# A 64-expert layer on one core: shared experts as split one-pass products in two halves, four memory rows per token

## The chip, the cores and the metric

The kernel runs on one core of a Trainium2 chip. The metric is the device time of one execution in microseconds (us). Its engines work side by side, each through its own list of instructions: PE (TensorE, matrix products), ACT (ScalarE), DVE (VectorE), POOL (GpSimd) and SP (SyncE, which only issues transfers). They wait for each other through semaphores. SBUF is the on-chip memory of 128 partitions, PSUM the banks that PE writes, DRAM the memory of the chip.

## The reference

A decoder of two layers on x of 4 x 512 tokens of width 512. The part that is changed is the feed-forward of the first layer:

```python
b, t, d = x.shape                      # B, T, D = 1, 512 x 4 tokens here, 512
E, K, F, S, SF, CAP = 64, 4, 128, 2, 512, 64
logits = flat @ router_w.T
scores = jax.nn.softmax(logits, axis=-1)
_, topk_idx = jax.lax.top_k(logits + router_bias, K)
topk_w = jnp.take_along_axis(scores, topk_idx, axis=-1)
topk_w = topk_w / topk_w.sum(axis=-1, keepdims=True)
# each expert takes its first CAP tokens: tok_table (E, CAP), w_table (E, CAP)
xg = flat[tok_table]
y = jnp.einsum('ecf,edf->ecd', silu(xg @ gate_w) * (xg @ up_w), down_w)
out = zeros.at[tok_table].add(y * w_table[..., None])
# two shared experts of width 512, for every token
sg = jnp.einsum('nd,sfd->nsf', flat, sh_gate_w)
su = jnp.einsum('nd,sfd->nsf', flat, sh_up_w)
out = out + jnp.einsum('nsf,sdf->nd', silu(sg) * su, sh_down_w)
x = layernorm(x + out)
```

Before it stand a gated linear recurrence and a layer of token-id experts, after it window attention, a product in an 8-bit format and a latent attention with eight experts.

## The kernel before

The program runs its stages one after the other; `moe_layer` is the third. Names in it: `B` = 4 groups of 512 tokens, 16 `TILES` of 128 tokens, `KD` = 4 slices of the width 512, `KF` = 4 slices of the shared width, `PAIRS` = 32 pairs of experts (two experts of 64 slots fill the 128 rows of one product), `K_C` = 4 experts per token.

*The shared experts.* Their work is cut into 64 steps, 8 for each of 8 units; a unit is one group of 512 tokens with one shared expert (`unit // SHARED` is the group). The first 4 steps of a unit are gate/up steps: 4 products of 128x512 for gate and 4 for up, in f32; ACT takes tanh of the gate (`shared_gate`), DVE makes the hidden product of it in two operations, `gu_s` and `hs`. The other 4 are down steps: 4 products each for one tile of 128 tokens, and one DVE operation that adds the result to that tile's rows (`row`). Steps 0 to 19 (`EARLY_STEPS`) come before the expert pairs, while the tokens are being routed; steps 20 to 47 are dealt out among the pairs (`middle`); steps 48 to 63 (`LATE`) come after the last pair.

*Routing.* For each group PE turns x (`turn_batch`, copied from PSUM by ACT into `xT`), computes the router's `logits`, and counts with `places` how many earlier tokens chose an expert. DVE does the rest in three parts: `pick` (four largest), `choose` (masks) and `share_out` (softmax weights, slots and addresses). POOL then writes 16 times 128 entries of (token, row of the sums, weight) into the table `slots` in DRAM by indirect transfers (L1210), four in flight at a time. The order on DVE is written out by hand: `share_out(2)` follows step 5, `share_out(3)` step 9, so that of the early steps 10 remain after it.

*The pairs.* When all 64 scatters have landed, SP reads the table back (`of_slot`, L1180), and POOL gathers for each pair its 128 rows of x (`gather`, L1222), two pairs ahead. On PE the loop is software-pipelined, with `middle` steps of the shared experts between:

```python
for q in range(-2, PAIRS + 1):
    if q + 2 < PAIRS: turn(q + 2)
    for n in middle.get(q, []): shared_step(n)
    if 0 <= q + 1 < PAIRS: gates(q + 1)
    if 0 <= q < PAIRS: turn_hidden(q)
    if 0 <= q - 1: down(q - 1)
```

The experts' weights come through a ring of four buffers of 1.5 MB; SP asks for pair q's when `down(q - 4)` is done. ACT scales a pair's result y by the slots' weights (`result`, L1297) and POOL scatters it with adding into `expert_sums` in DRAM (`add_rows`, L1230), two rows per token (a token's row is 2 * token + half, where half tells experts of one parity from the other's); each scatter waits for the one before. `expert_sums` is zeroed in the first stage by one transfer (L263).

*The end.* After the last scatter SP loads the sums in 6 transfers of up to three tiles (L1193), DVE adds the two rows of a token to its own (`sum_rows`, L1589 and L1590), takes mean and variance (`spread`), POOL the power -0.5, and ACT normalises. The tiles are taken between the late steps (`tiles_at`).

What sets the order is the text alone: each engine does its list as written, and there is no planner.

## Time and profile before

| | |
|---|---|
| time, median of 3 runs | 2373.93 us (2370.86 to 2379.55) |
| the profiled execution: its time | 2381.64 us |
| the profiled execution: its span | 2379.9 us |
| mean granted clock of PE | 0.951 |
| busy: PE, DVE, ACT, POOL | 90%, 57%, 34%, 28% of the span |
| the 64-expert stage | about 481 to 982 us of the span |
| its rows of the page: f32 products gate, up, down | 256 each, 115.4, 115.1 and 114.0 us busy |
| scatters with adding (L1230) | 32, of 1570 ns each on POOL |
| ring loads of 1536 KB | 32, 7.0 us from issue to landing |
| loads of the sums of 1536 KB | 5 (and a smaller one), 9.9 us |
| zeroing of the sums, 8192 KB | 1, 27.5 us |

Times inside the trace count from the start of the span. A window's row gives the busy time of each engine in a stretch and the number of its instructions; where PE's busy time equals the stretch, PE sets its length. The page counts a PE instruction as busy from its own start to a modelled end, and instructions overlap, so the step from one start to the next is read from the timeline instead. The granted clock is a share of full speed.

### The profile page before, as it was taken

The numbers are of one execution on the slowest core, as the hardware profiler recorded it, in microseconds if no ns is written. First come the engines' busy times: TensorE is split into PE (matmuls) and PEld (weight loads), VectorE is DVE, ScalarE is ACT, GpSimd is POOL, SyncE is SP. The second block draws the span as 40 slices with busy tenths as digits, with TensorE's granted clock in tenths as the row PEclk, the third lists the DMA queues.
The fourth block names the chain that finished last, engine by engine and source line by source line (L and its number), as shares of the span: only waits on it lengthen the run. The fifth ranks groups of instructions, "written<-read, shape, count | busy, mean of one in ns | idle before, by whom it ended". The sixth has DMA issues, their size and how long they took to land. (4 is left out here: it accounts for less than half of the span.)

```text
span 2379.9 us, 31463 instructions
## 1 busy us (share of the span) xinstructions
PE 2139.5 (90%) x10918; PEld 1180.7 (50%) x10919; DVE 1362.7 (57%) x3185; ACT 806.4 (34%) x1333; POOL 674.3 (28%) x945
## 2 busy tenths in 40 slices
PE   9999979979999999879999988578888888889994
PEld 5777748755444443445555543233333333336763
DVE  5866768846121226566777774845656565445443
ACT  5554624420112211333444433533322232123333
POOL 1200015516433321223343433011113131214553
PEclk9999989979999999998999997789999999999997
DMA  7211232270177764363333330200000000065555
GB/s 268 75 36 54 89 121 82 94 290 1 28 240 248 244 210 152 100 134 81 81 88 82 88 68 1 97 3 1 2 19 2 19 28 19 19 177 159 100 99 171
DMA packets 101178, 230.31 MB, mean 97 GB/s; under 512 B 18886, under 2 KB 42626, under 8 KB 93870
## 3 DMA queue, kind: packets, MB, share of 16 engines
q1 hardware_dynamic: 78478, 186.61, 25.3%
q0 software_dynamic: 22560, 41.87, 7.9%
q8 instruction: 83, 1.36, 0.2%
q14 instruction: 57, 0.47, 0.1%
HBM read 169.45 MB, written 63.53 MB: 98 GB/s over the span
## 5 line engine op out<-in xcount | busy, mean ns | idle before, releaser
L2137 DVE CUSTOM_DVE_ANT_0 D_ps<-D_ps,D_mask 128x256 f32<-128x256 f32 (+1 forms) x512 | 186.6, 419 | 61.9 <-PE D_ps L2033 60.6
L1859 POOL TENSOR_SCALAR_AFFINE_SELECT D_probs<-D_probs 128x256 f32<-128x256 f32 x256 | 106.4, 422 | 288.2 <-ACT D_probs L1917 288.1
L1917 ACT ACTIVATE D_probs<-D_ps 128x512 f32<-128x512 f32 (+1 forms) x256 | 125.4, 543 | 184.4 <-PE D_ps L2055 184.3
L3170 DVE TENSOR_REDUCE F_neg_max<-F_ps 128x4 f32<-128x2048 f32 (+1 forms) x64 | 93.9, 1488 | 107.3 <-PE F_ps L3068 101.2
L2920 ACT ACTIVATE F_probs<-F_ps 128x1536 f32<-128x1536 f32 (+1 forms) x48 | 76.4, 1591 | 186.9 <-PE F_ps L3084 186.9
L1393 PE MATMUL C_ps<-C_down_shared,C_hs 128*128 128x512 f32 x256 | 114.0, 594 | 2.5 <-DVE C_hs L1560 1.5
L1381 PE MATMUL C_ps<-C_xT,C_gate_shared 128*128 128x512 f32 x256 | 115.4, 593 | 0.5 <-ACT C_xT L1256 0.5
L1381 PE MATMUL C_ps<-C_xT,C_up_shared 128*128 128x512 f32 x256 | 115.1, 592 | 0.0
L2033 PE MATMUL D_ps<-D_k_stack,D_q_stack 96*128 96x256 bf16 (+1 forms) x512 | 94.2, 270 | 15.2 <-DVE D_maxima L2137 11.8
L1230 POOL DMA_INDIRECT expert_sums<-C_y,C_of_slot x32 | 50.2, 1570 | 173.0 <-ACT C_y L1297 107.9
L2801 POOL TENSOR_SCALAR_AFFINE_SELECT F_probs<-F_probs 128x512 f32<-128x512 f32 x64 | 41.1, 654 | 180.5 <-ACT F_probs L2920 180.5
L3486 POOL DMA_INDIRECT choice_sums<-G_y,G_sum_at x38 | 65.9, 1734 | 88.7 <-DMA choice_sums<-G_y,G_sum_at 76.2
L2055 PE MATMUL D_ps<-D_q_stack,D_k_stack 99*128 99x256 bf16 (+1 forms) x512 | 76.8, 276 | 14.8 <-DMA D_q_stack<-D_m_lo 14.8
L1210 POOL DMA_INDIRECT slots<-C_entry,C_address x64 | 66.0, 1031 | 76.4 <-DVE C_address L1545 40.1
L2072 PE MATMUL D_ps<-D_probs,D_v 128*32 128x256 f32 (+1 forms) x1024 | 78.6, 380 | 6.0 <-POOL D_probs L1861 3.3
L1381 PEld LDWEIGHTS C_ps<-C_xT,C_up_shared 128*128 128x128 f32 x256 | 48.6, 190 | 61.2 <-issue 61.0
L1861 POOL TENSOR_SCALAR_AFFINE_SELECT D_probs<-D_probs 128x256 f32<-128x256 f32 x192 | 78.8, 410 | 0.0
L1393 PEld LDWEIGHTS C_ps<-C_down_shared,C_hs 128*128 128x128 f32 x256 | 47.1, 190 | 57.2 <-issue 52.6
L2033 PEld LDWEIGHTS D_ps<-D_k_stack,D_q_stack 96*128 96x128 bf16 x512 | 39.4, 101 | 72.7 <-DVE D_maxima L2137 34.7
L1274 ACT ACTIVATE C_th_s<-C_ps 128x512 f32<-128x512 f32 x32 | 19.1, 597 | 165.0 <-PE C_ps L1381 165.0
L1381 PEld LDWEIGHTS C_ps<-C_xT,C_gate_shared 128*128 128x128 f32 x256 | 47.2, 190 | 54.2 <-issue 54.2
L1553 DVE SCALAR_TENSOR_TENSOR C_gu_s<-C_th_s,C_ps 128x512 f32<-128x512 f32 x32 | 22.0, 686 | 90.3 <-ACT C_th_s L1274 90.2
(574 smaller groups left out, 4947.7 us busy)
## 6 DMA issues: line engine op xcount, KB each, us to landing
C_ring<-moe_experts_dram SPq DMA_DIRECT2D x32, 1536.0 KB, 7.0
qk_parts<-D_parts SPq DMA_DIRECT2D x32, 384.0 KB, 2.6
expert_sums<-A_zeros SPq DMA_DIRECT2D x1, 8192.0 KB, 27.5
C_ring<-expert_sums SPq DMA_DIRECT2D x5, 1536.0 KB, 9.9
D_q_stack<-qk_parts SPq DMA_DIRECT2D x16, 384.0 KB, 4.7
D_k_stack<-qk_parts SPq DMA_DIRECT2D x16, 384.0 KB, 7.7
B_w<-ctxT_dram SPq DMA_DIRECT2D x1, 4096.0 KB, 16.8
B_c<-ctx_dram SPq DMA_DIRECT2D x4, 1024.0 KB, 8.2
```

What stands on the lines that cost most here:

```text
L1210: pool.indirect_dma_start(slots, bass.IndirectOffsetOnAxis(ap=address[:, b, k, t:t + 1], axis=0), entry[:, b * GROUP + t, k, :], None, bou ...
L1381: last = nc.tensor.matmul(ps[:, bank + part, :], w_shared[part][:, k, f:f + P], xT[:, k, g * S:(g + 1) * S], start=(k == 0), stop=(k == KD ...
L1393: last = nc.tensor.matmul(ps[:, 2 + c % 2, :], hs[:, m, i * P:(i + 1) * P], down_shared[:, s * KF + m, :], start=(m == 0), stop=(m == KF - 1))
L1859: last = nc.gpsimd.affine_select(now[:, :, 0:P], now[:, :, 0:P], [[0, 2], [1, P]], ALU.is_ge, 0.0, base=0, channel_multiplier=-1)
L1861: last = nc.gpsimd.affine_select(now[:, :, P:2 * P], now[:, :, P:2 * P], [[0, 2], [-1, P]], ALU.is_ge, 0.0, base=0, channel_multiplier=1)
L1917: nc.scalar.activation(probs[at % 2][:, 2 * pair:2 * pair + 2, 0:w], ps[:, 4 + unit % 3, :].rearrange("p (h q) -> p h q", h=2)[:, :, 0:w], ...
L2033: last = nc.tensor.matmul(ps[:, 2 + u % 2, h * 256 + first:(h + 1) * 256], q_stack[0:STACK, head, t * P:(t + 1) * P], k_stack[0:STACK, hea ...
L2055: last = nc.tensor.matmul(bank[:, h * 256:h * 256 + w], k_stack[:, head, kb * P:(kb + 1) * P], q_stack[:, head, kb * P:kb * P + w], start= ...
L2072: last = nc.tensor.matmul(ps[h * (P // 4):(h + 1) * (P // 4), 7, kb * P:kb * P + w], v[b % 2][:, kb, first:first + 2 * DK], probs[at % 2][ ...
L2137: last = nc.vector.tensor_tensor_reduce(now, now, mask[:, first:256], 1.0, -3e38, ALU.add, ALU.max, maxima[n % 2][:, head, t:t + 1])
L2920: nc.scalar.activation(probs[u][:], ps[:, 0:GROUP, 0:WIDTH[u]], ACT.Exp, scale=1.0 / np.sqrt(HD)).then_inc(exp_ready, 1)
L3170: last = nc.vector.tensor_reduce(neg_max[n % 2][:, :, t], ps[:, 0:GROUP, at:at + w], AX_X, ALU.max, negate=True)
```

## The change

The two shared experts are treated as one of width 1024, in two halves of 512: units 0 to 3 are the first half with groups 0 to 3, units 4 to 7 the second half (`half, g = divmod(unit, B)`).
SBUF holds the weights of one half at a time and x for two groups at a time. The second halves are loaded over the first between the ring's loads (q == 6 and 11), rounded at q == 6 and 10. x is written out to DRAM (`spill_x`, 2 MB for each of 4 groups) and brought back for the second half (`bring_x`).

The transposes of groups 2 and 3 move in between the early steps, and with them their logits, `pick`, `choose` and `share_out` move back. There are 24 early steps; the others are dealt out anew over the pairs.

`expert_sums` has four rows per token (4 * token + k), each written once, so the scatter neither adds nor waits for the one before; the zeroing is twice as large. At the end 16 loads of 1 MB replace 6 of up to 1.5 MB; POOL adds rows 2 and 3 to rows 0 and 1 (`halve`), then DVE adds both to the token's row as before.

The core of the diff:

```diff
@@ rglru_layer, SP
-                         zeros[:].unsqueeze(1).to_broadcast([P, 2 * TILES, D])).then_inc(zeroed, 16)
+                         zeros[:].unsqueeze(1).to_broadcast([P, K_C * TILES, D])).then_inc(zeroed, 16)
@@ moe_layer
-EARLY_STEPS = 20
+EARLY_STEPS = 24
...
-    for n in range(EARLY_STEPS, LATE):
-        middle.setdefault((n - EARLY_STEPS) * PAIRS // (LATE - EARLY_STEPS), []).append(n)
+    HALF = STEPS // 2
+    for n in range(EARLY_STEPS, HALF):
+        middle.setdefault(n - EARLY_STEPS + (-1 if n < HALF - KF else 0), []).append(n)
+    for n in range(HALF, LATE):
+        middle.setdefault(8 + (n - HALF) * (PAIRS - 8) // (LATE - HALF), []).append(n)
+    SECOND_GATES, SECOND_DOWN = 6, 10
...
@@ SP
+            def load_weights(half, *parts):
+                for part in parts:
+                    if half:
+                        sp.wait_ge((gate_s, up_s, down_s)[part], B * KF)
+                        sp.wait_ge(w_lo_ready[part], 1)
...
+                    sp.dma_start(w_raw[part][:], source).then_inc(w_in[part], 16)
+            def spill_x(b):
+                sp.wait_ge(x_hi_ready, KD * (b + 1))
+                sp.dma_start(x_spill[b, 0], x_hi[b % 2][:].bitcast(F32).rearrange("p k n -> p (k n)")).then_inc(spilled[b % 2], 16)
+                sp.wait_ge(x_lo_ready, b + 1)
...
+            def bring_x(g):
+                sp.wait_ge(up_s, (B + g - 1) * KF)
+                sp.wait_ge(spilled[g % 2], 2 * 32)
...
+            load_weights(0, 0, 1, 2)
             for q in range(RING):
...
+            for b in range(B):
+                spill_x(b)
             sp.wait_ge(scattered, 16 * K_C * TILES)
             sp.dma_start(of_slot[:].rearrange("p n o -> p (n o)"), slots.rearrange("(p n) o -> p (n o)", p=P)).then_inc(slots_in, 16)
+            bring_x(0)
             for q in range(RING, PAIRS):
+                if q == 6:
+                    load_weights(1, 0, 1)
+                    bring_x(1)
+                if q == 11:
+                    load_weights(1, 2)
+                if q == 16:
+                    bring_x(2)
+                if q == 28:
+                    bring_x(3)
...
+            for t in range(TILES):
+                if t >= HOMES:
+                    sp.wait_ge(summed, t - HOMES + 1)
+                sp.dma_start(homes[:, t % HOMES].rearrange("p c n -> p (c n)"),
+                             sums.rearrange("(t p c) d -> p t (c d)", p=P, c=K_C)[:, t, :]).then_inc(sums_in[t % HOMES], 16)
@@ POOL
             def add_rows(q):
                 pool.wait_ge(y_ready, q + 1)
-                if q >= 1:
-                    pool.wait_ge(stored[(q - 1) % 2], 16 * ((q - 1) // 2 + 1))
...
-                                        bounds_check=last_sum, oob_is_err=False, compute_op=ALU.add).then_inc(stored[q % 2], 16)
+                                        bounds_check=last_sum, oob_is_err=False).then_inc(stored[q % 2], 16)
+            def halve(t):
+                pool.wait_ge(sums_in[t % HOMES], 16 * (t // HOMES + 1))
+                nc.gpsimd.tensor_tensor(homes[:, t % HOMES, 0:2, :], homes[:, t % HOMES, 0:2, :], homes[:, t % HOMES, 2:4, :], ALU.add
+                                        ).then_inc(halved, 1)
@@ ACT
                 for k in range(KD):
                     act.wait_ge(x_turned, b * KD + k + 1)
-                    nc.scalar.copy(xT[:, k, b * S:(b + 1) * S], ps[:, 4 + k % 2, :]).then_inc(xT_ready, 1)
+                    nc.scalar.copy(x_raw[b % 2][:, k, :], ps[:, 4 + k % 2, :]).then_inc(x_raw_ready, 1)
+                    nc.scalar.copy(x_hi[b % 2][:, k, :], ps[:, 4 + k % 2, :]).then_inc(x_hi_ready, 1)
+            def high_of_hidden(m):
+                act.wait_ge(hs_raw_ready, m + 1)
+                nc.scalar.copy(hs_hi[:, m % KF, :], hs_raw[:, m % KF, :]).then_inc(hs_hi_ready, 1)
...
@@ PE
+                        pe.wait_ge(w_hi_ready[part], half + 1)
                         for k in range(KD):
-                            last = nc.tensor.matmul(ps[:, bank + part, :], w_shared[part][:, k, f:f + P],
-                                                    xT[:, k, g * S:(g + 1) * S], start=(k == 0), stop=(k == KD - 1))
+                            nc.tensor.matmul(ps[:, bank + part, :], w_hi[part][:, k, now], x_hi[j][:, k, :], start=(k == 0), stop=False)
...
+                            nc.tensor.matmul(ps[:, bank + part, :], w_hi[part][:, k, now], x_lo[j][:, k, :], start=False, stop=False)
...
+                            last = nc.tensor.matmul(ps[:, bank + part, :], w_lo[part][:, k, now], x_hi[j][:, k, :], start=False,
+                                                    stop=(k == KD - 1))
...
-            turn_batch(2)
-            turn_batch(3)
             pe.wait_ge(converted, 1)
             places(0)
             for n in range(EARLY_STEPS):
                 shared_step(n)
                 if n == 1:
                     places(1)
-                if n == 2:
+                if n == 4:
+                    turn_batch(2)
+                if n == 6:
                     logits(2)
-                if n == 5:
+                if n == 10:
                     places(2)
-                if n == 7:
+                if n == 12:
+                    turn_batch(3)
+                if n == 14:
                     logits(3)
-                if n == 9:
+                if n == 18:
                     places(3)
@@ DVE
+            def low_of_hidden(m):
+                dve.wait_ge(hs_hi_ready, m + 1)
+                nc.vector.tensor_tensor(hs_lo[:, m % KF, :], hs_raw[:, m % KF, :], hs_hi[:, m % KF, :].bitcast(F32), ALU.subtract
+                                        ).then_inc(hs_lo_ready, 1)
             def shared_step(n):
                 unit, down, i = step_of(n)
+                if i or down:
+                    if not down or i == 0:
+                        low_of_hidden(unit * KF + (KF if down else i) - 1)
...
             choose(0)
+            low_x(0)
             pick(1)
+            low_of_weights(0, 0, 1)
             share_out(0)
             shared_step(0)
             choose(1)
             shared_step(1)
             share_out(1)
+            low_of_weights(0, 2)
             shared_step(2)
...
+            low_x(1)
+            for n in range(3, EARLY_STEPS):
                 shared_step(n)
+                if n == 8:
+                    pick(2)
+                    low_x(2)
+                if n == 9:
+                    choose(2)
+                if n == 11:
+                    share_out(2)
+                if n == 16:
+                    pick(3)
+                    low_x(3)
+                if n == 17:
+                    choose(3)
+                if n == 19:
+                    share_out(3)
...
@@ program
-    expert_sums = nc.dram_tensor("expert_sums", (2 * TOKENS, D), F32).ap()
+    expert_sums = nc.dram_tensor("expert_sums", (K_C * TOKENS, D), F32).ap()
```

## Rows read from the trace of the kernel before

**Rows 1.** Windows: us, busy PE PEld DVE ACT POOL, clock, DMA share, GB/s

```profile
480.80:517.00 36.20, 27.55 (x131) 24.61 (x131) 12.25 (x51) 10.74 (x24) 0.34 (x3) 0.55 0.99 368
517.00:635.90 118.90, 117.96 (x327) 56.10 (x328) 63.89 (x171) 9.02 (x20) 67.93 (x66) 1.00 0.11 38
635.90:896.00 260.10, 257.15 (x1121) 115.85 (x1121) 52.55 (x136) 53.03 (x107) 76.54 (x60) 1.00 0.69 220
896.00:981.70 85.70, 83.15 (x194) 36.20 (x192) 52.74 (x104) 15.57 (x23) 6.84 (x6) 1.00 0.30 105
```

**Rows 2.** Timeline of PE, gate products of two steps: start, us, engine, line, operation

```profile
607.27 3.60 PE L1381 MATMUL C_ps<-C_xT,C_gate_shared 128*128 128x512 f32 x8
...
614.14 3.60 PE L1381 MATMUL C_ps<-C_xT,C_gate_shared 128*128 128x512 f32 x8
```

**Rows 3.** Timeline of PE, one-pass products in the first stage

```profile
213.63 1.33 PE L435 MATMUL A_ps<-A_u_lo,A_wa_hi 128*128 128x512 f32 x5
214.79 1.32 PE L429 MATMUL A_ps<-A_u_hi,A_wa_hi 128*128 128x512 f32 x5
```

**Rows 4.** Groups by line, later stages: busy us, mean ns, idle before

```profile
L2195 DVE TENSOR_TENSOR D_wv_lo<-D_wv,D_wv_hi 128x2048 fp32r<-128x2048 f32 x1 | 2.3, 2293 | 1.1 <-ACT D_wv_hi L1934 1.1
...
L3528 ACT CAST G_x_hi<-G_xgT 128x512 fp32r<-128x512 f32 x38 | 23.6, 620 | 7.1 <-DVE G_xgT L3753 6.5
...
L3759 DVE TENSOR_TENSOR G_x_lo<-G_xgT,G_x_hi 128x512 fp32r<-128x512 f32 x38 | 26.3, 693 | 24.8 <-ACT G_x_hi L3528 24.7
```

**Rows 5.** Timeline of PE, the second group's logits

```profile
502.50 7.09 PE L1353 MATMUL C_ps<-C_router,C_xT 128*128 128x64 f32 x32 [0.68 <-ACT C_xT L1256]
```

**Rows 6.** Timeline of DVE: first operations of share_out(0), choose, step 1, share_out(1), step 2

```profile
512.05 1.23 DVE L1517 TENSOR_TENSOR C_picked<-C_chosen,C_expd 128x1024 f32<-128x1024 f32 x1
...
524.93 0.17 DVE L1497 CAST C_at<-C_best_at 128x16 f32<-128x16 uint32 x1
...
529.22 0.69 DVE L1553 SCALAR_TENSOR_TENSOR C_gu_s<-C_th_s,C_ps 128x512 f32<-128x512 f32 x1
...
531.79 1.22 DVE L1517 TENSOR_TENSOR C_picked<-C_chosen,C_expd 128x1024 f32<-128x1024 f32 x1
...
539.51 0.68 DVE L1553 SCALAR_TENSOR_TENSOR C_gu_s<-C_th_s,C_ps 128x512 f32<-128x512 f32 x1
```

**Rows 7.** Timeline from the last group's first scatter to the first gather

```profile
600.23 0.97 POOL L1210 DMA_INDIRECT slots<-C_entry,C_address  x1 [1.39 <-DMA slots<-C_entry,C_address]
...
624.76 0.33 SPq L1180 DMA_DIRECT2D C_of_slot<-slots  x1
...
627.25 0.98 POOL L1222 DMA_INDIRECT C_xg<-x,C_of_slot  x1 [3.64 <-DMA C_of_slot<-slots]
```

**Rows 8.** DMA issues, the gathers: median us from issue to landing

```profile
C_xg<-x,C_of_slot POOLq DMA_INDIRECT x32, 5.1
```

**Rows 9.** Windows with full queues and in the middle of the pairs

```profile
910.00:925.00 15.00, 15.00 (x36) 6.63 (x35) 10.17 (x20) 1.19 (x2) 0.00 (x0) 1.00 0.99 397
...
700.00:750.00 50.00, 50.00 (x218) 22.60 (x216) 9.46 (x25) 10.90 (x22) 17.87 (x14) 1.00 0.88 282
```

**Rows 10.** Windows in the second stage, PE idle and the 4 us after

```profile
334.00:346.00 12.00, 0.34 (x2) 0.34 (x3) 1.91 (x5) 0.00 (x0) 4.85 (x6) 0.57 0.59 219
346.00:350.00 4.00, 4.00 (x15) 3.25 (x14) 1.38 (x2) 1.17 (x2) 0.68 (x2) 0.58 0.82 191
```

**Rows 11.** Timeline of SP, the issue of the loads of the sums

```profile
908.44 23.52 SPq L1193 DMA_DIRECT2D C_ring<-expert_sums  x6
```

**Rows 12.** Timeline of POOL and DVE, two additions that overlap

```profile
1660.96 1.27 POOL L2795 TENSOR_TENSOR F_plain<-F_raw,F_rope 128x512 f32<-128x512 f32 x1 [5.46 <-ACT F_raw L2860]
1661.59 1.18 DVE L3153 TENSOR_TENSOR F_full<-F_full,F_plain 128x512 f32<-128x512 f32 x1
```

**Rows 13.** Group of DVE's first additions of the sums in the last stretch

```profile
L1589 DVE TENSOR_TENSOR rows<-rows,C_ring 128x512 f32<-128x512 f32 x16 | 11.0, 689 | 4.6 <-DMA C_ring<-expert_sums 4.2
```

**Rows 14.** Waits of SP's queue after the zeroing: us in all, count, longest

```profile
SPq L252 <- PE A_ps L435: 114.1, 2, 61.6
```

More of the change, by code:

```diff
@@ L1085, in moe_layer @@
     LATE = STEPS - LATE_UNITS * 2 * KF
-    LOADS = [range(i, min(i + 3, TILES)) for i in range(0, TILES, 3)]
+    HOMES = 6
     def step_of(n):
@@ L1132, in moe_layer @@
         share, place, kept, slotf, drop = (sb(n, [P, K_C, GROUP]) for n in ("share", "place", "kept", "slotf", "drop"))
-        sloti, pairi, half = (sb(n, [P, K_C, GROUP], I32) for n in ("sloti", "pairi", "half"))
-        twice = sb("twice", [P, TILES], I32)
+        sloti, pairi = (sb(n, [P, K_C, GROUP], I32) for n in ("sloti", "pairi"))
         address = sb("address", [P, B, K_C, GROUP], I32)
@@ L1266, in shared_gate @@
                 unit, down, i = step_of(n)
+                if i or down:
+                    if not down or i == 0:
+                        high_of_hidden(unit * KF + (KF if down else i) - 1)
                 if not down:
@@ L1366, in shared_step @@
                 unit, down, i = step_of(n)
-                g, s = divmod(unit, SHARED)
+                half, g = divmod(unit, B)
+                j = g % 2
                 if not down:
@@ L1385, in shared_step @@
                     c = unit * KF + i
-                    if n == KF:
-                        pe.wait_ge(down_in, 16)
+                    now = slice(i * P, (i + 1) * P)
                     if c >= 2:
                         pe.wait_ge(added, c - 1)
+                    pe.wait_ge(w_hi_ready[2], half + 1)
                     for m in range(KF):
-                        pe.wait_ge(hs_ready, unit * KF + (m + 1 if i == 0 else KF))
-                        last = nc.tensor.matmul(ps[:, 2 + c % 2, :], hs[:, m, i * P:(i + 1) * P],
-                                                down_shared[:, s * KF + m, :], start=(m == 0), stop=(m == KF - 1))
+                        pe.wait_ge(hs_hi_ready, unit * KF + (m + 1 if i == 0 else KF))
+                        nc.tensor.matmul(ps[:, 2 + c % 2, :], hs_hi[:, m, now], w_hi[2][:, m, :], start=(m == 0), stop=False)
+                    pe.wait_ge(w_lo_ready[2], half + 1)
+                    for m in range(KF):
+                        nc.tensor.matmul(ps[:, 2 + c % 2, :], hs_hi[:, m, now], w_lo[2][:, m, :], start=False, stop=False)
+                    for m in range(KF):
+                        pe.wait_ge(hs_lo_ready, unit * KF + (m + 1 if i == 0 else KF))
+                        last = nc.tensor.matmul(ps[:, 2 + c % 2, :], hs_lo[:, m, now], w_hi[2][:, m, :], start=False, stop=(m == KF - 1))
                     last.then_inc(down_s, 1)
@@ L1604, in _ @@
             nc.vector.memset(so_far[:], 0.0)
-            nc.vector.tensor_scalar(twice[:], myself[:], 2, None, ALU.mult)
+            for k in range(K_C):
+                nc.vector.tensor_scalar(entry[:, :, k, 1], myself[:], K_C, k, ALU.mult, ALU.add)
             nc.vector.tensor_copy(entry[:, :, :, 0], myself[:].unsqueeze(2).to_broadcast([P, TILES, K_C]))
```

180 lines of the change are left out of this document (108 added, 72 removed).

## The prediction

> **What bounds the kernel now.** I read the page's shares first (PE 90% busy), then the windows of the 64-expert stage, since an average over stages says nothing of one. The reader is to see that PE is the limit in three of its four stretches [rows 1]: 117.96 of 118.90 us busy in the early one, 257.15 of 260.10 in the one with the expert pairs, 83.15 of 85.70 in the last. Only the front, 36.20 us with DMA at a share of 0.99, waits for data. So a cheaper product shortens a stretch only as far as nothing else becomes late in it. The chain of waits ends in the latent stage and does not reach this one; I therefore took the order of the work on each engine from the code and the durations from the timeline and the groups by line, and last looked for what the trace shows of a DMA at its limit and of POOL beside DVE.
>
> **The change part by part.** *The products.* A gate/up step of 16 f32 products takes 614.14 - 607.27 = 6.87 us [rows 2], a down step of 8 half of it, 3.43. Five f32r products of the same shape take 214.79 - 213.63 = 1.16, or 0.233 each [rows 3]. So 24 of them are 5.59, 12 are 2.80: 1.28 and 0.63 less. With 32 steps of each kind PE has 61 us less to do. Where that is worth something is the question in each stretch.
>
> *Front and early steps: +45.* Each group's logits need both copies of x (0.62 each on ACT [rows 4]); I put the end of logits(1), 502.50 + 7.09 = 509.59 before [rows 5], at 512.5, two pairs of copies of 1.46 later. From there DVE's list is serial: pick 2.3 (2.46 from 509.59 to 512.05, less the signal [rows 5, 6]), two lows of weights 4.6 (2.29 each [rows 4]), share_out 7.7 (531.79 to 539.51 [rows 6]), step 0 1.4, choose 4.3 (524.93 to 529.22 [rows 6]), step 1 2.1, share_out 7.7, low of down 2.3, step 2 2.1, low of x 2.3, step 3 2.1; a step is two operations, from step 1 on three, of 0.69 [rows 4]. That is 38.9: DVE is through step 3 at 551.4, and with the rounding on ACT and the wait signals PE begins step 4 at 552.3. PE's own steps 0 to 3 are 22.4, so it waits some 13 us there, before the first down step.
> Steps 4 to 19 are 8 x 5.59 + 8 x 2.80 = 67.1, the logits of groups 2 and 3 7.4 (7.09 at a clock near half, about 3.6 at full, an estimate [rows 5]), their transposes, moved in from the front, 7.0 (per group four of the eight copies of 0.62 before PE may fill the banks again, and its own 1.0), places 0.6. Step 12 needs the low of step 11's result, which stands on DVE behind share_out(2): 6.5 of its 7.7 show. Less 0.7 hidden under the copies: 87.9, step 19 ends at 640.2. Now comes what I hold to be the main loss: share_out(3) stands behind step 19 (before: step 9). Its addresses are there at 640.2 + 0.9 + 7.7 = 648.8. The 16 scatters of a group took 624.76 - 600.23 = 24.5 [rows 7]; SP's load of the slots follows at once, the gather 2.5 later (627.25), and a gather lands 5.1 after its issue [rows 8]. Turn(0) comes at 648.8 + 24.5 + 2.5 + 5.1 = 680.9 instead of 635.9. PE has only steps 20 to 23 (11.2) to cover it, is done at about 658 and idles 23. Bounds: without any of the waits on DVE the early steps end 15 us earlier (+30); with the clock falling in each wait, as below, +54.
>
> *Pairs: -23.7.* 12 gate steps x 1.28 and 12 down steps x 0.63 save 15.4 and 7.6, and the early part has taken over four down steps: 13.7. Sum 36.7. The turns, gates and downs of the pairs themselves stay as they are. Against the gain: between gates(5) and gates(6) SP must now also bring the second gate and up halves and a group of x, 2 x 1.05 and 2 x 1.05 MB beside ring loads of 1.57 MB each: 7.3 MB at the 397 GB/s seen with the queues full [rows 9] is 18.5 us and about 2 of latency, against some 14 us of PE's work that covers it (three pairs' own 3.7, that is 257.15 less 12 x 6.87 and 16 x 3.43 over 32, and a down step): 7 us. The x of groups 2 and 3 costs about 1.5 each, for the ring is four deep and refills behind it. And PE comes out of its 23 us of idling at a low clock: after 12 us with hardly any PE work the granted clock was 0.57, near the lower of its two levels (1.2 of 2.4 GHz), and the next 4 us ran at 0.58 although PE was busy throughout [rows 10]; that is about 2 us lost after each long wait, 3 in all. -36.7 + 10 + 3 = -23.7. In total the stretch must carry 44.0 (ring) + 3.1 + 8.4 (x) + 8.4 (gathers) + 8.4 (scatters) = 72.3 MB: 182 us at 397 GB/s, but 226 at 320 GB/s, the rate that a full share would have given in the middle of the pairs (282 at 0.88 [rows 9]). So ends: -36.7 (nothing waits) to 0 (no more than the 282 itself: 256 us, and the clock's 3). I take -23.7, near the end that the chain of PE's own work gives, since at the share of 0.88 PE was busy for all 50.00 of 50.00 us; the scatters without adding need no wait for the one before and cost nothing here, since y's release is hidden behind PE.
> The Trainium skill ("SBUF — State Buffer", "Summary: rules for kernel authors") reckons 358 GB/s between HBM and SBUF; the row of 397 differs and decides. By the page's figure the 7.3 MB would take 20.4 us, an estimate, and the sum would be 2 us higher.
>
> *Late steps: +20.3.* The scatters end sooner: no chain of waits, so the first sums can be asked for some 8 us after the last pair instead of 12.4 (908.44 - 896.0 [rows 1, 11]). A tile is 1 MB now, POOL halves it: twice the elements of its 128x512 addition of 1.27 [rows 12], 2.5 us; the first tile is ready at about +13. Then there are 16 halvings = 40.5 and 32 additions on DVE of 0.69 = 22 [rows 13], the lows of hidden 3.4. When POOL and a DVE operation with two SBUF inputs run at once they do not share: the DVE addition that began 0.63 us into POOL's 1.27 took 1.18 instead of 0.69, that is, it ended 0.54 after POOL had [rows 12, 13]. Taken as exclusion the three add up to 66, with DVE's remaining work between to 75; from the last tile's sum to the end of the stage are 18 for the last down steps, spreads and normalising. 13 + 75 + 18 = 106 against 85.7. Bounds: if POOL and DVE share, PE alone is left, with 8 x 1.28 + 8 x 0.63 = 15.3 less to do (-15); if every halving also delays the gate steps' operations that PE waits for, 16 x 1.0 more, +36. The 16 MB of sums need 42 us at 397 GB/s and stay under POOL's pace.
> The Trainium skill ("SBUF — State Buffer", "Who interferes with whom") says that a DVE operation with two SBUF inputs and a GpSimd one that reads SBUF hold the shared read for the whole instruction, whoever begins first. The row of 1.18 agrees; were the price always that row's 0.49, 40 such operations would cost 20 us, and late would come to +11.
>
> *The rest.* Zeroing doubles to 16 MB: by the page 8 MB landed in 27.5 us; SP's next step after it has a wait of 61.6 us [rows 14], which hides 27.5 more. Weights' first halves are 3 MB less ahead of the ring in the front; it stays with the transposes and ACT.
>
> Sum: +45 - 23.7 + 20.3 = +41.6, to the profiled execution's 2381.64: 2423.2. The median of the runs shown, 2373.93, lies 7.7 below that execution, so I predict 2416.
>
> **The rivals.** *POOL and DVE share after all.* For it: 1.18 is one row, and tiles may queue so that the two alternate. Against it: all 16 halvings fall into the stretch with 32 additions. Then a quarter of PE's 15.3 shows in the late steps, no more, for DVE's 52.74 [rows 1] grow by 5.5 of lows and stand right behind PE: -4, sum +17.3: 2391. *DMA binds the pairs.* For: share 0.88 in the middle already [rows 9] and now 72.3 MB in 236.4 us, 306 GB/s where 220 were asked for [rows 1]. Against: the 397 with big transfers. At 282 the stretch goes to about 260 instead of 236.4: 2440. *Gains and waits cancel.* DVE's early list is half as costly as I make it and the pairs keep 33 of their 36.7: +25 - 33 + 8: 2374. *Faster.* One mechanism: PE alone decides. Its place is turn(0); it decides as soon as steps 4, 12 and 20 find their operands ready. Then only the distance of share_out(3) from turn(0) is left (32 us of scatters, load and gather against 11.2 of PE's work, +22), the pairs give all 36.7 and the late steps 10 of their 15.3: -25, about 2349. For it: PE is the limit in three stretches now. Against it: DVE's list of 38.9 us beside 22.4 of PE's work.
>
> **How the numbers follow.** Forecast 0.40 (2416, alone 2400 to 2432); POOL and DVE share 0.22 (2391); DMA binds 0.12 (2440); cancel 0.13 (2374); faster 0.13 (2349). The range is 2352 to 2445: it leaves out about half of the faster case and half of the DMA case. Within 0.5%, some 12 us, a measurement can't tell from no change. The cancelling case is the one that lies there; so faster 0.13, same 0.13, slower 0.74.
>
> **What would show it.** The products: step time 5.6 on PE with f32r. Early: PE idle before the first down step released by DVE's lows or ACT's hs, share_out(3) ending near 649, and PE idle before turn(0) released by the gather, some 23 us. Pairs: idle before gates(6) released by the ring's DMA, none elsewhere over 3 us. Late: halvings of 2.5 us or more, DVE additions of up to 3 us that end just after a halving, the last tile's sum about 88 us after the last pair. I am wrong if turn(0) comes before 660, if additions stay at 0.69 beside POOL, or if the pairs' stretch keeps its 260.

## The result, and the profile after

The changed kernel takes 2433.92 us (median of 4 runs, 2424.17 to 2443.09), the kernel before beside it 2375.30: 1.0246 times as long, with an interval of 1.0201 to 1.0292. That is 18 us more than the 2416 forecast and inside the range. The profiled execution took 2443.09 us, the longest of the four.

I cut the stage at four starts on PE: its first transposes, turn(0), the down products of the last pair, and the next stage's first product. The lengths between them, in us, for every kernel of this study; each ratio is to runs of the kernel before that were timed beside that kernel, whose median moves by a few us (2372.78 beside e10, 2377.56 beside e9):

| kernel | front and early, to turn(0) | pairs | last stretch | time, median | ratio to before |
|---|---|---|---|---|---|
| before | 149.1 | 259.1 | 92.1 | 2375.30 | |
| changed | 196.2 | 252.2 | 107.6 | 2433.92 | 1.0246 |
| e1 routing earlier | 172.1 | 251.4 | 107.9 | 2412.67 | 1.0162 |
| e2 DVE halves | 196.5 | 250.9 | 105.1 | 2429.36 | 1.0213 |
| e3 loads spread | 193.5 | 238.7 | 105.9 | 2419.06 | 1.0177 |
| e4 two rows again | 195.9 | 267.9 | 92.2 | 2429.51 | 1.0232 |
| e5 four rows alone, on before | 139.9 | 259.1 | 102.8 | 2386.30 | 1.0045 |
| e6 = e2, order of sums | 195.0 | 255.6 | 96.6 | 2420.85 | 1.0190 |
| e7 = e1 + e3 | 171.9 | 240.1 | 106.7 | 2396.51 | 1.0092 |
| e8 all, and two more edits | 166.7 | 230.3 | 97.4 | 2373.80 | 0.9992 |
| e9 = e8, four tiles on PE | 166.7 | 228.3 | 99.0 | 2372.54 | 0.9982 |
| e10 = e9, last sums earlier | 167.3 | 227.0 | 94.9 | 2370.11 | 0.9982 |

So the changed kernel loses 47.1 us before turn(0), gains 6.9 in the pairs and loses 15.5 in the last stretch: +55.7; 1.9 more come ahead of the stage and 3.6 after it, which makes the 61.1 between the two spans (2441.0 and 2379.9). Each length is of one execution. Where kernels of the table share a stretch's instructions, it differs by up to 3.0 us in the first column (changed, e2, e3, e6), 4.7 in the second (changed, e1, e2, e6) and 2.0 in the third (changed, e1, e3, e7), so a smaller difference shows nothing. What follows the stage takes 1383.8 to 1396.4 us in them, though nothing was changed in it.

The windows of the three stretches of the changed kernel, columns as in [rows 1], which they answer:

```profile
488.60:684.80 196.20, 143.60 (x633) 117.36 (x633) 101.15 (x239) 39.54 (x75) 66.65 (x66) 0.82 0.32 122
684.80:936.95 252.15, 226.18 (x1229) 141.21 (x1229) 64.46 (x147) 64.64 (x122) 59.84 (x60) 0.95 0.72 264
936.95:1044.57 107.62, 75.74 (x293) 58.80 (x293) 82.16 (x117) 21.40 (x33) 48.25 (x24) 0.83 0.41 161
```

PE fills none of the three any more: it idles 52.6, 26.0 and 31.9 us. Its products did get cheaper. Two gate steps that follow each other on its timeline (start, duration) are 5.44 us apart, where [rows 2] have 6.87:

```profile
943.53 1.07 PE L1471 MATMUL C_ps<-C_x_hi,C_gate_hi 128*128 128x512 f32 x4
...
948.97 1.07 PE L1471 MATMUL C_ps<-C_x_hi,C_gate_hi 128*128 128x512 f32 x4
```

PE's waits in the early part, in order: for choose(1), for the last hidden product before the first down step, for the lows behind share_out(2) and share_out(3), and for the first gather:

```profile
532.59 0.40 PE L1448 MATMUL C_ps<-C_mask,C_before 128*128 128x256 bf16 x1 [5.71 <-DVE C_so_far L1612]
...
551.16 0.80 PE L1490 MATMUL C_ps<-C_down_hi,C_hs_hi 128*128 128x512 f32 x1 [3.74 <-ACT C_hs_hi L1327]
...
602.76 0.80 PE L1496 MATMUL C_ps<-C_down_hi,C_hs_lo 128*128 128x512 f32 x1 [5.21 <-DVE C_hs_lo L1660]
...
651.56 0.80 PE L1496 MATMUL C_ps<-C_down_hi,C_hs_lo 128*128 128x512 f32 x1 [5.21 <-DVE C_hs_lo L1660]
...
684.78 1.11 PE L1506 MATMUL C_ps<-ident,C_xg 128*128 128x128 f32 x4 [22.60 <-DMA C_xg<-x,C_of_slot]
```

The chain to that gather, from the timelines of DVE, POOL and SP, answers to [rows 7]: last address at 650.72, first scatter, table, first gather 28 us after the address.

```profile
650.72 0.17 DVE L1646 TENSOR_TENSOR C_address<-C_sloti,C_drop 128x16 int32<-128x16 int32 x1
```

```profile
651.66 0.97 POOL L1256 DMA_INDIRECT slots<-C_entry,C_address  x1 [24.38 <-DVE C_address L1646]
...
678.64 0.98 POOL L1268 DMA_INDIRECT C_xg<-x,C_of_slot  x1 [3.70 <-DMA C_of_slot<-slots]
```

In the pairs PE has three long waits for the ring. Its timeline, with one product that did not wait (755.66) between; the trace names no releaser ("issue"), but SP's timeline, below it, shows what stood ahead of the ring's load:

```profile
747.28 3.68 PE L1517 MATMUL C_ps<-C_ring,C_xgT 128*64 128x256 f32 x16 [10.29 <-issue]
...
755.66 1.95 PE L1517 MATMUL C_ps<-C_ring,C_xgT 128*64 128x256 f32 x16
...
825.82 3.68 PE L1517 MATMUL C_ps<-C_ring,C_xgT 128*64 128x256 f32 x16 [5.38 <-issue]
...
912.13 3.21 PE L1517 MATMUL C_ps<-C_ring,C_xgT 128*64 128x256 f32 x14 [4.58 <-issue]
```

```profile
723.13 0.38 SPq L1198 DMA_DIRECT2D C_gate_raw<-moe_sh_gate_dram  x1
723.61 0.45 SPq L1198 DMA_DIRECT2D C_up_raw<-moe_sh_up_dram  x1
724.15 2.56 SPq L1209 DMA_DIRECT2D C_x_hi<-x_spill  x1
726.76 1.69 SPq L1210 DMA_DIRECT2D C_x_lo<-x_spill  x1
...
806.46 0.38 SPq L1209 DMA_DIRECT2D C_x_hi<-x_spill  x1
...
893.69 0.38 SPq L1209 DMA_DIRECT2D C_x_hi<-x_spill  x1
```

After such a wait the same 16 products take 3.68 us instead of 1.95, as in [rows 10]: the granted clock was 0.50 in the 4 us from 747.28, after 10.29 us of idling, and 1.00 from 751.30 on. In the last stretch DVE's additions of the sums take up to 2.77 us while POOL halves, and 0.68 when it does not (POOL's list pauses from 968.4 to 972.6); these rows, from the timelines of POOL and DVE, answer to [rows 12, 13]:

```profile
946.69 7.67 POOL L1291 TENSOR_TENSOR C_homes<-C_homes 128x1024 f32<-128x1024 f32 x3 [6.70 <-DMA C_homes<-expert_sums]
954.92 13.45 POOL L1291 TENSOR_TENSOR C_homes<-C_homes 128x1024 f32<-128x1024 f32 x5 [0.56 <-DMA C_homes<-expert_sums]
```

```profile
949.96 2.15 DVE L1707 TENSOR_TENSOR rows<-rows,C_homes 128x512 f32<-128x512 f32 x1
952.15 2.77 DVE L1708 TENSOR_TENSOR rows<-rows,C_homes 128x512 f32<-128x512 f32 x1
...
969.97 0.68 DVE L1707 TENSOR_TENSOR rows<-rows,C_homes 128x512 f32<-128x512 f32 x1
```

### The profile page after: what moved, and what is told of

Same layout as the page of the kernel before. It is cut to its first block and busy times, and to the rows that moved or that the text cites. A ratio compares the mean times of both kernels' runs of the same rounds, so it can differ in the third digit from the quotient of the medians.

```text
span 2441.0 us, 32391 instructions
## 1 busy us (share of the span) xinstructions
PE 2098.7 (86%) x11299; PEld 1266.2 (52%) x11303; DVE 1427.1 (58%) x3222; ACT 841.3 (34%) x1387; POOL 695.4 (28%) x961
## 5 line engine op out<-in xcount | busy, mean ns | idle before, releaser
L1517 PE MATMUL C_ps<-C_ring,C_xgT 128*64 128x256 f32 x512 | 67.3, 408 | 22.2 <-issue 20.5
L1273 POOL DMA_INDIRECT expert_sums<-C_y,C_of_slot x32 | 32.6, 1019 | 167.4 <-ACT C_y L1371 167.4
L2265 DVE DVE_READ_ACCUMULATOR2_ANT D_maxima<- 128x1 f32 x512 | 72.6, 142 | 0.0
L3781 PE MATMUL G_ps<-G_w_down,G_hidT 128*128 x152 | 71.5, 593 | 0.9 <-ACT G_hidT L3663 0.9
L2183 PEld LDWEIGHTS D_ps<-D_q_stack,D_k_stack 99*128 99x128 bf16 x512 | 42.7, 101 | 52.5 <-issue 23.0
L3127 PE MATMUL F_ps<-F_wo,F_oT 128*128 128x512 f32 x128 | 63.3, 622 | 6.0 <-DVE F_raw L3344 3.0
L1685 DVE SCALAR_TENSOR_TENSOR rows<-C_ps,rows 128x512 f32<-128x512 f32 x32 | 22.1, 691 | 78.4 <-PE C_ps L1496 76.4
L2145 PE MATMUL D_ps<-D_wo,D_oT 128*128 128x512 f32 x128 | 66.5, 621 | 0.2 <-ACT D_oT L2034 0.2
L1490 PE MATMUL C_ps<-C_down_hi,C_hs_hi 128*128 128x512 f32 x128 | 42.5, 442 | 27.3 <-ACT C_hs_hi L1327 26.3
```

What stands on the lines that cost most here:

```text
L1517: last = nc.tensor.matmul(ps[e * CAP:(e + 1) * CAP, 5, 0:2 * F_C], xgT[q % 2][:, k, e * CAP:(e + 1) * CAP], ring[q % RING][:, e, k * 2 * F ...
L2145: last = nc.tensor.matmul(ps[:, bank, :], oT[t][:, k, :], wo[:, k, :], start=(k == 0), stop=(k == KD - 1))
L2183: last = nc.tensor.matmul(bank[:, h * 256:h * 256 + w], k_stack[:, head, kb * P:(kb + 1) * P], q_stack[:, head, kb * P:kb * P + w], start= ...
L2265: last = nc.vector.tensor_tensor_reduce(now, now, mask[:, first:256], 1.0, -3e38, ALU.add, ALU.max, maxima[n % 2][:, head, t:t + 1])
L3781: last = nc.tensor.matmul(ps[:, 6 + a, :], hidT[a][:, m, :], w_down[:, bass.ds(e, 1), m, :], start=(m == 0), stop=(m == MF - 1))
```

## The experiments

**e1: the routing of groups 2 and 3 earlier.** Shown for group 3; group 2 and `exponentials` on ACT move likewise.

```diff
@@ PE
-                if n == 14:
+                if n == 13:
                     logits(3)
-                if n == 18:
+                if n == 15:
                     places(3)
...
@@ DVE
-                if n == 16:
+                if n == 13:
                     pick(3)
...
-                if n == 17:
+                if n == 14:
                     choose(3)
-                if n == 19:
+                if n == 15:
                     share_out(3)
...
```

> Only the order of the routing of groups 2 and 3 changes: logits, pick, choose and share_out of group 2 after steps 5, 5, 6 and 7, of group 3 after steps 13, 13, 14 and 15 (in the changed kernel after 6, 8, 9, 11 and 14, 16, 17, 19). Theory: turn(0) waits for the last group's addresses, which stood behind step 19. Then the addresses are there some 30 us earlier (about 620), the waits for lows at steps 12 and 20 (6.5 each) go, PE's idle time before turn(0) falls from 22.6 to under 10 us, turn(0) comes near 654 instead of 684.8, and the kernel is about 30 us faster than the changed one (2404). Rival: the gain is given back in the pairs' loads, since the ring's transfers bind there: then the pairs' stretch grows from 253 by what turn(0) gains, and the kernel stays within 8 us of 2434.

Turn(0) came 24.1 us nearer to the stage's start (196.2 to 172.1), not 30, and PE still waits 11.4 there, more than the 10 I allowed: the steps before it became shorter by the same edit, so there was less to cover the scatters. The pairs kept their length (251.4), with the first wait for the ring as long as ever. The theory holds in its cause and overstated the size: the median is 21.3 us below the changed kernel's, where 30 were expected. The rival falls. The rows, PE's timeline of e1:

```profile
660.15 1.11 PE L1506 MATMUL C_ps<-ident,C_xg 128*128 128x128 f32 x4 [11.39 <-DMA C_xg<-x,C_of_slot]
...
722.53 3.68 PE L1517 MATMUL C_ps<-C_ring,C_xgT 128*64 128x256 f32 x16 [10.24 <-issue]
```

**e2: DVE halves.**

```diff
@@ DVE, sum_rows; POOL's halve goes
-dve.wait_ge(halved, t + 1)
+dve.wait_ge(sums_in[t % HOMES], 16 * (t // HOMES + 1))
+steps.after(nc.vector.tensor_tensor(homes[:, t % HOMES, 0:2, :], homes[:, t % HOMES, 0:2, :], homes[:, t % HOMES, 2:4, :], ALU.add))
```

> Only who halves the four rows changes: DVE adds rows 2 and 3 to rows 0 and 1 itself (one 128x1024 operation of about 1.25 us a tile) and POOL does nothing but the powers. Theory: POOL's halving and DVE's additions exclude each other, so moving the work to the engine that waits costs less than it frees: the additions fall from up to 2.77 us to 0.69, the last stretch from 102 to 85 to 95 us, the kernel is 8 to 17 us faster than the changed one. Rival: POOL's help is real and DVE becomes the bound: 16 x 1.25 = 20 us more on DVE, the last stretch grows by 5 to 15.

Neither came: the last stretch went from 107.6 to 105.1. The groups of DVE by line, of the changed kernel and then of e2 (busy us, mean ns), say why:

```profile
L1708 DVE TENSOR_TENSOR rows<-rows,C_homes 128x512 f32<-128x512 f32 x16 | 23.4, 1466 | 0.5
L1707 DVE TENSOR_TENSOR rows<-rows,C_homes 128x512 f32<-128x512 f32 x16 | 20.1, 1254 | 0.4
```

```profile
L1696 DVE TENSOR_TENSOR C_homes<-C_homes 128x1024 f32<-128x1024 f32 x16 | 19.6, 1223 | 0.4
L1697 DVE TENSOR_TENSOR rows<-rows,C_homes 128x512 f32<-128x512 f32 x16 | 11.1, 692 | 0.6
L1698 DVE TENSOR_TENSOR rows<-rows,C_homes 128x512 f32<-128x512 f32 x16 | 11.1, 692 | 0.5
```

Beside POOL the additions are busy 43.5 us, alone 22.2: POOL's 41 us of halving cost DVE 21.3, and doing it itself costs DVE 19.6. POOL's help is worth next to nothing: the 2.5 us are little more than the 2.0 by which equal stretches differ. What both kernels share is DVE's one list, which in e2 runs for 70.8 us (946.81 to 1017.64) with one gap of 0.59.

**e3: the second half's loads spread over the ring.**

```diff
@@ SP
                 if q == 6:
-                    load_weights(1, 0, 1)
-                    bring_x(1)
+                    load_weights(1, 0)
+                if q == 7:
+                    load_weights(1, 1)
                 if q == 11:
                     load_weights(1, 2)
-                if q == 16:
-                    bring_x(2)
-                if q == 28:
-                    bring_x(3)
+                if q in (13, 15):
+                    bring_x(1, (q - 13) // 2)
+                if q in (17, 20):
+                    bring_x(2, (q - 17) // 3)
...
+            bring_x(3)
             sp.wait_ge(y_in_psum, PAIRS)
```

The second argument of `bring_x` picks the rounded part (0) or the rest (1).

> Only the places of the second half's loads between the ring's loads change: gate at ring load 6, up at 7, x of group 1 in two parts at 13 and 15, of group 2 at 17 and 20, of group 3 after the last ring load (in the changed kernel 4.2 MB at load 6, 2.1 MB each at 16 and 28). Theory: the three waits for the ring in the pairs (10.3, 5.4 and 4.6 us) come from these lumps, while the mean rate of 264 GB/s leaves room. Then they fall to under 6 us together, the pairs' stretch from 253 to about 236, and the kernel is 13 to 18 us faster than the changed one. Rival: the transfers bind the stretch as a whole (72 MB): the waits only move to other pairs, and it gains less than 6 us.

The pairs went from 252.2 to 238.7. PE's waits for the ring, as the view of waits counts them (us in all, times, longest), are 9.3 us in six pieces; in the changed kernel they were 20.5 in four, up to 10.3:

```profile
PE C_ps L1520 <- issue: 9.3, 6, 2.2
```

The 9.3 is more than the 6 I allowed, but the stretch gained 13.5, more than the waits alone lost (11.2): PE's busy time fell as well, from 226.2 to 223.7 us, with a mean granted clock in the pairs of 0.98 instead of 0.95. A window around e3's pairs:

```profile
681.00:921.00 240.00, 224.56 (x1232) 140.59 (x1232) 64.48 (x147) 64.68 (x122) 60.53 (x61) 0.98 0.76 279
```

The rate rose to 279 GB/s, so the places and sizes of the loads, not the total of bytes, held the pairs up.

**e4: two memory rows again, in the changed kernel.** The loads of the sums, `sum_rows`, the row numbers and the zeroing are those of the kernel before, and so is `add_rows`; POOL's `halve` goes.

```diff
                 pool.wait_ge(y_ready, q + 1)
+                if q >= 1:
+                    pool.wait_ge(stored[(q - 1) % 2], 16 * ((q - 1) // 2 + 1))
...
-                                        bounds_check=last_sum, oob_is_err=False).then_inc(stored[q % 2], 16)
+                                        bounds_check=last_sum, oob_is_err=False, compute_op=ALU.add).then_inc(stored[q % 2], 16)
```

> The memory rows are as in the kernel before (two rows a token, scatters that add and wait for each other, 6 loads of the sums, two DVE additions a tile, zeroing of 8 MB); products, halves and routing order as in the changed kernel. Theory: the last stretch loses to the halving beside DVE, so without it the stretch is at or below the 85.7 of before, since its products are 15.3 us shorter: 78 to 86 instead of 102, and the kernel 15 to 24 us faster than the changed one; turn(0) and the pairs stay within 3 us. Rival: the lows and the rounding of the hidden product make the last stretch long, not the rows: then it stays above 95.

The last stretch fell by 15.4 to 92.2, so the four rows cost there all that the stretch had lost. But it did not go below the stretch of before, though PE has 15 us less to do: PE waits 14.4 us for hidden products that stand behind DVE's sums, and DVE's first sum itself waits 7.9 us for its load, which comes after the last adding scatter. The waits of PE and of DVE there:

```profile
PE C_ps L1490 <- ACT C_hs_hi L1327: 14.4, 3, 6.2
DVE rows L1711 <- DMA C_ring<-expert_sums: 7.9, 1, 7.9
```

And the pairs, where I expected nothing, grew by 15.7, so that the median is 4.4 us below the changed kernel's and not 15 to 24. The waits of POOL, then of PE, in the pairs of e4:

```profile
POOL expert_sums L1284 <- DMA expert_sums<-C_y,C_of_slot: 92.4, 18, 8.9
```

```profile
PE C_ps L1506 <- DMA C_xg<-x,C_of_slot: 42.2, 11, 22.7
```

A scatter that waits for the one before holds POOL for 92 us, the gathers queue behind it, and PE waits for them ten times (42.2 less the 22.7 at turn(0): 19.5 us). A scatter lands 6.9 us after its issue in e4 and 6.8 in the changed kernel (medians), so the transfer itself is hardly longer; but adding and waiting were put back together, and no run tells the two apart.

**e5: the four rows alone, on the kernel before.** The same functions as in e4, the other way round, with POOL's `halve`:

```diff
-                                        bounds_check=last_sum, oob_is_err=False, compute_op=ALU.add).then_inc(stored[q % 2], 16)
+                                        bounds_check=last_sum, oob_is_err=False).then_inc(stored[q % 2], 16)
```

> The kernel before with the memory rows alone changed: four rows a token, scatters without adding or waiting, 16 loads of 1 MB, POOL halves; f32 products, one x for all groups and the routing order stay. Theory: before, PE sets the pairs (257 of 260 us busy), so the scatters' waits are hidden there and their going gives nothing (within 2 us); the last stretch (92.1 from the last pair to the next stage's first product) grows, since DVE's 53 us of work become about 74 beside a PE that needs 83: +5 to +13; the kernel is 5 to 13 us slower than before. Rival: the scatters without adding free POOL and DMA in any kernel, as they do with the f32r products, where two rows cost the pairs 16 us: then the pairs shrink by 5 or more and the whole is no slower than before.

The theory holds: the pairs keep 259.1, the last stretch grows by 10.7, and the kernel is slower by 9.3 us (2386.30 beside 2376.98), 1.0045 (1.0021 to 1.0068). DVE's additions are busy 42.1 us there too. Its front was 9 us shorter in the profiled execution, by the granted clock (last section). e4 and e5 together: scatters that neither add nor wait are worth 15.7 us beside the cheap products and nothing beside the f32 ones.

**e6: one tile of sums after each late step** (on e2).

```diff
-tiles_at = {1: (0, 1), 2: (2, 3), 3: (4, 5), 4: (6,), 5: (7,), 6: (8,), 7: (9,), 8: (10, 11)}
+tiles_at = {r: (r - 1,) for r in range(1, 11)}
+tiles_at[11] = (10, 11)
...
-                if n == LATE + 9:
-                    for t in range(12, TILES):
-                        sum_rows(t)
                 if n >= LATE + 12:
-                    spread(n - LATE)
+                    whole(n - LATE)
```

> The changed kernel with DVE halving (as in e2) and one tile of sums after each late step instead of two after each of the first three and the tiles 12 to 15 in a lump. Theory: the last stretch is bound by DVE's one list, which in e2 was busy without a gap for 70 us and then idled while PE did the last steps; spread evenly, PE's last steps lie beside it: the stretch falls from 105 (last pair to next stage) to 88 to 96, and the kernel is 9 to 17 us faster than e2 (2429). Rival: the sums' arrival or PE's own chain sets the end: less than 4 us.

Not shown: what normalises the tiles (`shifts` on DVE, its counterpart on ACT) moves back with them. The stretch went from 105.1 to 96.6, and the kernel is 8.5 us faster than e2, both just short of what was named. The order of DVE's list is a term of its own.

**e7: the edits of e1 and e3 together.**

> The edits of e1 (routing earlier) and e3 (loads spread) together in the changed kernel. Theory: they mend different waits and add up: 24.6 at turn(0) and 13.5 in the pairs, 2434 - 37 = 2397 (2392 to 2402). Rival: pairs that start earlier meet the same transfers, so part is given back: 2403 or more.

2396.51: they add up (37.4 us less than the changed kernel, alone 21.3 and 14.9).

**e8: the edits of e1, e2, e3 and e6, and two more.**

```diff
-EARLY_STEPS = 24
+EARLY_STEPS = 26
...
             shared_step(1)
-            share_out(1)
             low_of_weights(0, 2)
             shared_step(2)
-            low_x(1)
             for n in range(3, EARLY_STEPS):
                 shared_step(n)
+                if n == 4:
+                    share_out(1)
+                if n == 5:
+                    low_x(1)
```

> All edits so far on the changed kernel, and two more: share_out(1) and the low of x of group 1 go behind step 4 and 5 on DVE (places(1) behind step 3 on PE), and there are 26 early steps. Theory: DVE's serial list before step 4 shortens by 10 us, all of the routing comes 10 us earlier, two more steps cover the wait at turn(0): turn(0) at about 645 with under 4 us of waiting; pairs 230 to 240, last stretch 88 to 96: 2361 to 2381 in all, about the kernel before (2375). Rival: steps taken out of the pairs leave the ring's transfers uncovered, and the pairs keep their 239 or more: 2382 to 2395.

2373.80, no different from before (0.9968 to 1.0015). PE waits 0.94 us at turn(0), and the pairs have 230.3, so the rival falls; they are shorter than e7's by 9.8, about the two gate steps that left them (2 x 5.44). But turn(0) came at 654, not 645, and the last stretch at 97.4 was above its range. This row of PE's timeline stands where the 22.60 stood:

```profile
654.31 0.63 PE L1498 MATMUL C_ps<-ident,C_xg 128*128 128x128 f32 x4 [0.94 <-DVE C_hs_raw L1671]
```

**e9: the sums of tiles 8 to 11 on PE** (on e8).

```diff
@@ PE, down steps of unit 6
+for r in range(K_C):
+    last = nc.tensor.matmul(ps[:, 2 + c % 2, :], two_ident[:], homes[:, at % HOMES, r, :], start=False, stop=(r == K_C - 1))
```

> e8 with the memory rows of tiles 8 to 11 summed on PE: four f32 products of 128x512 with twice the identity go into the PSUM bank of the tile's own down step, so that DVE's one operation there adds them as well; DVE sums 12 tiles instead of 16. Theory: the last stretch is still bound by DVE's list (75.6 of 89.4 us busy in e8), and PE has room: 4 x 2.6 = 10.5 us less on DVE, 16 x 0.86 = 13.8 more on PE, of which 70 were busy. The last stretch falls from 97.4 (last pair to next stage) to 90 to 93, the kernel to 2366 to 2371 where e8 had 2374: faster than before by 0.2 to 0.4%. Rival: with 84 us of products PE becomes the bound and nothing is gained: 2372 to 2378.

Not shown: the order of the loads, which changes with it. The stretch did not shorten (99.0), and the time, 2372.54, lies in the rival's range. Its reason is not what the rows show, for PE was not full: it waited 4.0 us in its steps instead of some 13, was busy 8.9 us longer (81.8), and stood idle at the end about as long as in e8, because DVE still had four sums to do behind the last downs. The rows are the next stage's first product, in e8 and then in e9:

```profile
981.99 1.94 PE L2100 MATMUL D_ps<-ident,rows 128*128 128x128 f32 x8 [11.41 <-PEq L92]
```

```profile
980.95 1.94 PE L2120 MATMUL D_ps<-ident,rows 128*128 128x128 f32 x8 [13.23 <-PEq L92]
```

**e10: those four sums after steps 57 to 60** (on e9).

```diff
                 if n >= LATE + 12:
-                    whole(n - LATE)
+                    spread(n - LATE)
+                if LATE + 9 <= n < LATE + 13:
+                    sum_rows(n - LATE + 3)
```

> e9 with the sums of tiles 12 to 15 on DVE after steps 57 to 60 instead of after the last four down steps. Theory: in e9 PE no longer waits in the last steps (4.0 us in all) but stands idle for 13.2 us after its last product, because four sums of 2.6 us follow the last downs on DVE; drawn ahead they lie beside PE's gate steps. PE's idle time at the end falls to 5.4 (as before the change), the last stretch from 99.0 to 91 to 93, the kernel to 2363 to 2368 (e9: 2372.5). Rival: the sums hold up the hidden products of steps 57 to 59 and PE waits there for as long: 2370 or more.

```profile
977.26 1.94 PE L2122 MATMUL D_ps<-ident,rows 128*128 128x128 f32 x8 [5.35 <-PEq L92]
```

The idle end is 5.35 as expected, but the stretch, 94.9, and the time, 2370.11, are both above the ranges named, and the time lies at the edge of the rival's. PE's waits in its steps rose from 4.0 to 6.2 us, so the rival's reason is there in part; it accounts for 2.2 of the 7.9 us that the idle end gave back. The time is 0.9982 of before, interval 0.9966 to 0.9999, so it beats the kernel before by hardly more than can be measured. In the profiled executions its pairs are 32.1 us shorter and its last stretch 2.8 longer, but the part before turn(0) takes 18.2 back. That would be 11.1 us, where the medians differ by 2.7. The profiled execution of the kernel before (2381.64) lies some 6 to 8 us above its medians; where the rest goes was not shown.

## Why the prediction was right, and which term was off

*Early, +45: measured +47.1.* Every wait that the working named is there: the one up to the first down step (5.71 at places(1) and 3.74 at the step; I had some 13), two lows behind share_out (5.21 each; I had 6.5), and the gather at turn(0), 22.60 where I had 23. These are 42.5 of PE's 52.6 us of idling; the rest is small waits. The last address came at 650.72 (648.8), turn(0) at 684.78 (680.9), in a stage that began 1.9 later. e1 shows the cause of half of it: the routing moved earlier, and 24.1 us came back. That DVE's list is behind the rest is read from the rows; e8 moves more of that list, but together with other edits.

*Pairs, -23.7: measured -6.9.* This is the term that was mis-sized. The mechanism was named and in the right places, gates(6) first, but "about 1.5 each" for the x of groups 2 and 3 were 5.4 and 4.6, and the 7 at gates(6) were 10.3: 20.5 us instead of 10. So the sign "none elsewhere over 3 us" failed. Of the remaining 6.3 of the 16.8, some 2.5 are other small waits, and some 4 that PE was busy longer than reckoned, at a granted clock of 0.95 instead of 1.00. e3 gave back 13.5 by moving loads alone. By the time alone, 2433.92, the rival "DMA binds the pairs" (2440) was nearer than the forecast (2416, alone 2400 to 2432). It named the stretch but not the cause: it took 282 GB/s as what the queues can carry there, and they moved 264 in the changed kernel, 279 in e3 with the same bytes and 294 in e10.

The scatters were put at nothing, and from the kernel before to the changed one that holds. In the kernel before, POOL waits 53.0 us in the pairs for the preceding scatter, as the line below shows, but PE is busy 256.2 of 259.1 us beside it, and e5 gains nothing by leaving these waits out; in the changed kernel they are gone.

```profile
POOL expert_sums L1230 <- DMA expert_sums<-C_y,C_of_slot: 53.0, 11, 5.8
```

What I had not asked is what they would cost if they stayed beside a PE with 36.7 us less to do: 15.7 (e4), and the pairs would have been 8.8 longer than before. That is where the expectation of e4 missed, not a term of this sum.

*Last stretch, +20.3: measured +15.5.* The exclusion is there (2.77 instead of 0.69), and e4 takes 15.4 back by leaving the four rows out. They have no fixed price: beside the f32 products they cost 10.7 (e5), and in e4 the 15.3 us that PE has less to do there brought nothing. Nor is blocking the only way in which they cost this: in e2 nothing blocks DVE, and the stretch is 2.5 shorter, because the halving then fills its list. POOL's halving itself is hardly stretched, 2.57 us on average, near the 2.5 estimated from [rows 12]. The time that DVE is blocked, 21.3 us, is near the 20 of the flat price of 0.49, by which I had +11; full exclusion gave +20.3, and the stretch lies between.
The Trainium skill ("SBUF — State Buffer", "Who interferes with whom") says that whoever begins first holds the shared read for the whole instruction and that the other one is blocked. DVE's additions of up to 2.77 us agree. POOL pays less than that rule gives: its halvings average 2.57 us against 2.42 for the one at 1003.73, which began ahead of DVE's addition, so not the 0.69 of a whole addition each; how the two take turns was not shown. "POOL and DVE share after all" is ruled out.

*Zeroing, +0:* the stage began 1.9 us later than before, and it begins between 486.1 and 488.6 us in all the profiled kernels, those with 8 MB (before and e4: 486.7 and 487.2) and those with 16 MB alike. No cost of it is seen.

In the profiled executions the sum was 61.1 against 41.6: the pairs' 16.8, 2.1 in the early part, 5.5 outside the stage, less 4.8 in the last stretch. The 5.5 have no known cause, and that the last stretch came out below its term was luck for the sum. The rivals "gains and waits cancel" and "faster" needed the waits of the early part to be missing, and these rows show them.

## What to carry to other kernels

When the bounding engine gets cheaper work, list every wait that it hid until then: the scatters' chain, the transfers in the ring and the other engine's list all came up here, and each took a part. A load that is put into a ring should be no larger than the ring's slack at that place; the same bytes in smaller pieces and at other places cost 9.3 us of waiting here instead of 20.5. Before work is given to a second engine, see whether the first one's operations grow beside it: here POOL's 41 us saved DVE nothing.

## What the runs showed of the hardware

The granted clock of the stage's front differs from one execution to another of nearly the same instructions. Two windows, of the profiled executions of the kernel before and of e5 (columns as in [rows 1]; the clock is the third last number):

```profile
490.00:513.00 23.00, 21.56 (x99) 19.78 (x98) 9.45 (x42) 5.80 (x13) 0.00 (x0) 0.50 1.03 397
```

```profile
490.00:513.00 23.00, 19.49 (x133) 15.44 (x132) 15.96 (x66) 9.80 (x24) 0.00 (x0) 0.97 1.04 398
```

In the one PE ran at the lower of its two levels (1.2 GHz) throughout, in the other nearly always at the higher (2.4 GHz), after an idle time of 12.97 and 12.85 us. That is where the 9 us between their early parts come from: up to turn(0) PE is busy 145.5 and 135.4 us with 457 instructions in each, and idles 3.7 and 4.5. It may also be why 20 runs of the kernel before, timed beside e5, lie as far apart as 2367.79 and 2381.61; this was not shown, and what decides the clock there stays open. In all other profiled kernels of the table it was between 0.50 and 0.58 in this window.
